# Query-key products of a chunked RWKV-7 block on Trainium2: two column tiles of 64 keys, or four of up to 32

## What is computed

```python
xn = layernorm(x)
# r, w, k, v, kk, a from xn by mixing with the row before, projections and low-rank terms
def step(S, inp):                       # S: 64 x 64 state
    rt, dt, kt, vt, at, bt = inp        # at = -kk, bt = kk * a, dt = exp(w)
    sa = einsum('bhij,bhj->bhi', S, at)
    S = S * dt[:, :, None, :] + sa[..., None] * bt[:, :, None, :] + vt[..., None] * kt[:, :, None, :]
    y = einsum('bhij,bhj->bhi', S, rt)
    return (S, y)
y = groupnorm(scan(step)) * ln_w + ln_b + bonus(r, k, v)
s = (y * g) @ w_output.T
out = x + s * silu(ffn(xn))
```

## Time and profile before

| | us |
|---|---|
| median of 3 runs | 1610.01 |
| lowest, highest | 1604.13, 1610.34 |
| span of the profiled execution | 1603.4 |
| TensorE matmuls busy in it | 1520.5 |
| TensorE weight loads busy | 1064.9 |
| VectorE busy | 1243.6 |
| ScalarE busy | 1069.5 |
| GpSimd busy | 354.6 |

### The profile page before, as it was taken

One profiled execution on the slowest core, in us unless ns is written; L12 is line 12 of the kernel. 1 busy time (PEld: TensorE's weight loads), 2 busy tenths in 40 slices (PEclk: granted clock), 3 DMA queues, 4 the chain that ended last, 5 costly groups with the idle time before them and its releaser, 6 DMA issues.

```text
span 1603.4 us, 48245 instructions
## 1 busy us (share of the span) xinstructions
PE 1520.5 (95%) x20288; PEld 1064.9 (66%) x20288; DVE 1243.6 (78%) x2661; ACT 1069.5 (67%) x1889; POOL 354.6 (22%) x362
## 2 busy tenths in 40 slices
PE   3699999999999999999999999999999999999887
PEld 1366767576676757667676676757667675766765
DVE  2968787787878878887887878778787887888643
ACT  3758586685857758685775858668585775768512
POOL 3121402313040131302213140231304013130201
PEclk9799999999999999999999999999999999999999
DMA  4011110301212021111202111030121202111020
GB/s 149 14 25 29 33 34 16 62 18 32 43 25 47 16 55 25 33 34 24 56 16 39 42 34 34 16 62 19 33 42 25 48 16 55 25 33 34 12 56 28
DMA packets 251430, 57.85 MB, mean 36 GB/s; under 512 B 223696, under 2 KB 250704, under 8 KB 251088
## 3 DMA queue, kind: packets, MB, share of 16 engines
q1 hardware_dynamic: 241936, 41.95, 13.9%
q10 hardware_dynamic: 9280, 12.81, 2.2%
HBM read 36.38 MB, written 18.35 MB: 34 GB/s over the span
## 4 chain that ended last, share of the span: by engine, by line
PE 92%; DVE 3%; ACT 2%; issue 1%; POOL 0%; DMA 0%; SPq 0%; ACTq 0%; DVEq 0%; POOLq 0%
PE bank L534 23%; PE chunk L380 15%; PE bank L544 11%; PE bank L509 8%; PE bank L664 4%; PE chunk L642 3%; PE chunk L614 3%; PE chunk L589 3%; PE chunk L598 2%; PE bank L485 2%; PE bank L380 2%; PE bank L517 2%; PE bank L479 2%; PE chunk L628 2%; DVE VU L981 1%
## 5 line engine op out<-in xcount | busy, mean ns | idle before, releaser
L1325 POOL TENSOR_TENSOR SF<-ST,CT 128x256 f32<-128x256 f32 x128 | 99.7, 779 | 728.8 <-DVE ST L1211 728.8
L534 PE MATMUL bank<-xT,wg 128*128 128x256 f32 x768 | 197.2, 391 | 14.2 <-DVE VU L981 13.5
L534 PE MATMUL bank<-xT,wu 128*128 128x256 f32 x768 | 207.3, 395 | 0.0
L544 PE MATMUL bank<-wd,hT 128*128 128x256 f32 x768 | 176.8, 383 | 1.9 <-DVE hT L1171 1.9
L534 PEld LDWEIGHTS bank<-xT,wg 128*128 128x128 f32 x768 | 136.3, 189 | 57.6 <-DVE VU L981 24.1
L544 PEld LDWEIGHTS bank<-wd,hT 128*128 128x128 f32 x768 | 143.3, 190 | 29.3 <-issue 7.2
L534 PEld LDWEIGHTS bank<-xT,wu 128*128 128x128 f32 x768 | 135.1, 188 | 34.8 <-issue 14.5
L380 PE MATMUL chunk<-KS,W 128*128 128x512 f32 x320 | 149.6, 598 | 0.3 <-ACT gT L719 0.3
L509 PE MATMUL bank<-qpad,KS 128*64 128x32 f32 x4096 | 141.2, 226 | 4.0 <-DVE KE L1143 4.0
L887 ACT ACTIVATE Y<-chunk 32x256 f32<-32x256 f32 x256 | 96.3, 376 | 70.9 <-PE chunk L598 67.0
L509 PEld LDWEIGHTS bank<-qpad,KS 128*64 128x64 f32 x4096 | 130.7, 141 | 14.1 <-issue 9.0
(11 more groups left out here) (156 smaller groups left out, 3231.3 us busy)
## 6 DMA issues: line engine op xcount, KB each, us to landing
smalls<-in_x SPq DMA_DIRECT2D x32, 256.0 KB, 3.1
Y<-in_x SPq DMA_DIRECT2D x32, 256.0 KB, 3.0
out<-fsil ACTq DMA_DIRECT2D x32, 256.0 KB, 2.6
scrA<-AM SPq DMA_DIRECT2D x64, 64.0 KB, 1.9
hat<-scrB SPq DMA_DIRECT2D x32, 128.0 KB, 3.1
hat<-scrF SPq DMA_DIRECT2D x32, 128.0 KB, 3.1
KE<-scrA SPq DMA_DIRECT2D x64, 32.0 KB, 2.2
scrT<-KE SPq DMA_DIRECT2D x16, 128.0 KB, 1.7
```

The source lines that it names most:

```text
L534: q = pe.matmul(o[:, TT_ * n2:TT_ * n2 + TT_], w[:, h, 128 * (n + n2):128 * (n + n2) + 128], x_now[:, h], start=(h == 0), stop=(h == NH - 1))
L544: q = pe.matmul(o[:, 256 * m:256 * m + 256], hT[:, n, 128 * m:128 * m + 128], wd[:, n, :], start=(n == 0), stop=(n == NF - 1))
L1325: pool.tensor_tensor(SF[:, :, :, :], ST[:, :, :, :], fade[:, c].unsqueeze(3).to_broadcast([128, B, NH, N]), ALU.mult).then_inc(*faded.up)
```

## The change

Each product is split by kind of key. Instead of one with 64 weight columns there are two, x = 0 and x = 1, whose results start at partitions 64b and 64b + 32: four column tiles of the array instead of two. Each loads only the keys up to the end of its query group, 8, 16, 24 or 32 columns, where 64 were loaded before. Streamed columns, the result's place in PSUM for every entry that the mask lets through, the mask and the order strings are as before. Result rows beyond the loaded keys are no longer written and keep what the bank held; the mask drops them.

```diff
-                                oc = o[64 * b:64 * b + 64, 128 * n:128 * n + 128].rearrange("p (x e) -> p x e", e=L)
-                                q = pe.matmul(oc[:, :, BL * j:BL * j + BL], K[:, 2 * n + b, 64 * j:64 * j + 64],
-                                              Q[:, 2 * n + b, j, :, :, :].rearrange("p a b e -> p (a b) e"), start=True, stop=True)
+                                for x in range(2):
+                                    p0, keys = 64 * b + L * x, BL * j + BL
+                                    oc = o[p0:p0 + keys, 128 * n:128 * n + 128].rearrange("p (x e) -> p x e", e=L)
+                                    q = pe.matmul(oc[:, :, BL * j:BL * j + BL], K[:, 2 * n + b, 64 * j + L * x:64 * j + L * x + keys],
+                                                  Q[:, 2 * n + b, j, :, :, :].rearrange("p a b e -> p (a b) e"), start=True, stop=True)
```

## The result

The changed kernel takes 1629.4 us (median of 4 runs, 1626.8 to 1646.8) where the kernel before takes 1610.2 beside it: ratio 1.0155, 95% interval 1.0123 to 1.0186. It is 1.5% slower (the ratios here compare the means of the runs, so they can differ by a few tenths of a per cent from the ratio of the medians, 1.012 in this case). The forecast was 1581, 1.8% faster, with a range of 1561 to 1602. The profiled execution took 1631.2 us, 1629.7 of it span, 26.3 more than the profiled one of before.

What follows compares the result with a forecast made beforehand. TensorE, 92% of the chain, was taken as the bound, its waves set by 64-column loads. Fourteen middle sections gave 26.6 us, the last 1.6, the first 1: 29 off 1610.0 gives 1581 us, range 1561 to 1602.

Steps and rivals of the forecast that it cites:

- the 58 ns: Products before the change: each wave of two starts takes 58 ns, set by loading 64 weight columns, 0.83 ns each.
- The wave after: Changed products: four tiles run together, 32 ns a wave; a half takes 0.64 us, a turn 1.15.
- the one for all tiles together: Matmul starts: 25 ns minimum taken across all tiles, 1.6 us per half, a kernel some 85 us slower.
- Rival D: Changed products: four column tiles over one row group don't run at once; 1622 or 1638 us, chance 0.12.
- Rival A: Short loads and streams: a fixed time per tile keeps waves between 32 and 58 ns; 1590 to 1604 us, chance 0.16.
- The walk: One middle section, followed through PE's waits for ACT and DVE: 1.9 us of 3.4 saved comes through.
- I take 0 in the sum: Fetching and issuing 8192 more instructions: priced at 0, with bounds of 0 and 0.9 us per half.
- C: Rival, changed products: nothing gained, wave near 58 ns by issue or half-overlapping tiles; 1604 to 1616 us, chance 0.07.
- The row of 32 starts: Two interleaved groups at 634.94 to 635.39: 32 starts in 0.45 us, taken to prove 64 instructions in that time.
- The trace shows no bound on that: Instruction fetch and issue: no limit seen against a half needing 128 instructions in 0.64 us instead of 64 in 1.06.
- the raw gain: Shorter halves and turns before waits: 3.4 us per tile of rows, 54 us over 16.
- The signs that were to show it: 8192 starts on L511, shorter halves, PE idle before L630, L591, L519 (0.1 to 0.5 us), sections 1.9 us shorter.

Runs made afterwards that it cites:

- v_trim64: Kernel before, still two column tiles, loading only key columns up to the mask's edge of kind 1 (40, 48, 56 or 64 instead of 64): 1592.1 us, ratio 0.9883.
- e_kind0: Changed kernel with only kind 0's products, kind 1's left out and its mask rows cleared, so the result is not the reference's: 1582.0 us, ratio 0.9831.
- a_after: The changed kernel, unaltered, measured a second time on another chip: 1641.3 us, ratio 1.0203 of the kernel before.

## Why the prediction was wrong, point by point

**What bounds the kernel, and the 58 ns: right.** A load's columns set the wave above 32 columns (v_trim64: 0.89 us a half, as computed from 0.83 ns a column).

**The wave after: right.** Waves of four start 29 to 32 ns apart in the first half shown above (their first starts at 640.127, .159, .188, .217), where 32 was forecast; a half takes 0.67 us at the median of the undisturbed ones (forecast 0.64), a turn 1.35 (forecast 1.15, partly by waits: the shortest is 1.21). Four column tiles over the same rows do run side by side, with starts 7 to 8 ns apart. Of the two readings of the Trainium skill's 25 ns between starts (TensorE: Matmul & The Clock Gate, section "Wait — 56ns, not 53.3ns?"), the one for all tiles together is refuted here. Rival D, that the tiles do not overlap, is refuted too, though the time fell into its range: its place was the array, and the array was fast. Rival A, a floor per tile between 32 and 58 ns, is also out.

**The walk and its sum of 29 us: right where the instructions allow it.** e_kind0, with about the array time of the forecast and the old number of instructions, takes 1582.0 us against the 1581 forecast, is 25 us (by the ratio 27) faster than its kernel before against 29 forecast, gains 1.9 us a section, and has its leads within 0.07 us of the walk's at each of the six places. Its halves were 0.05 us shorter than forecast and it uses two tiles, so it tests the walk and the waits, not the overlap of four tiles, which the halves of the changed kernel show.

**"I take 0 in the sum": the step that failed.** It stands under "What else is edited", as the price of 8192 more instructions, with bounds of 0 and 0.9 us per half, from 64 instructions seen in 0.45 us. What it cost was 38.3 us of standstills, and by the balance below some 10 us more at half clock behind them, against a gain of 27; the upper bound, "near no saving", was too low as well, and among the rivals only C named issue, with nothing gained at most (1604 to 1616). The row of 32 starts proves how fast instructions that are already there can be issued. It says nothing of how fast new ones arrive: 64 instructions are a quarter of a piece, and the limit is one piece in 2.7 to 3.7 us, some 11 to 14 ns an instruction, over a stretch of several us. "The trace shows no bound on that" was wrong as well. The q8 row was there (162 packets of 16.4 KB), and so were two idle times of 0.35 us ended by "issue" in the middle of groups, each after a piece that had been used up in 3.3 to 3.4 us. The kernel before ran just at the edge: four of its pieces pass in under 3.4 us; of after's, 52 do.

**The balance.** Against the profiled execution of before, in us of span: the array's gain as e_kind0 shows it, 1.9 a section, -27; 32 standstills, +38.3; half clock, 34.4 us instead of 14.0 after the first 95, at most half of the difference, +10 (an estimate); and the start, which was 4.3 us later in this execution before the first product of the change had run (L494, the last TensorE group ahead of them, stands at 72.01 instead of 67.72):

```profile
72.01 1.98 PE L494 MATMUL bank<-KS,con 64*64 64x512 f32 x8 [7.77 <-DVE KS L1062]
```

Together +26, measured 26.3 (L494 stands at 67.7 to 74.6 us in the twelve profiled executions, and before's is the earliest). This adds terms as if they did not touch one another, which is rough: while TensorE stands, the other engines get ahead, and a part of the waits that ate the raw gain in e_kind0 falls away. Behind the third half TensorE is idle before L591 for 0.14 us in after, 15 times, and for 0.25 us in e_kind0; before L519 it is 0.32 at most against 0.45.

The medians differ by only 19 us and the means by 25. Before's profiled execution, the early starter, was 6.6 us under its median, and after's was 1.8 us over.

**The signs that were to show it.** 8192 starts on L511, DVE and ACT unchanged: seen. New idle times before L591 and L519: seen, but smaller than forecast (0.14 us and up to 0.32), and none before L630 that before did not have. Each section 1.9 us shorter: not seen, the median is 96.2 us against 95.1.

## What to carry to other kernels

Where a change splits tensor instructions into more and shorter ones, count the instructions that pass in any 3.5 us, not only those of a group: here TensorE got 256 in 2.7 to 3.7 us, and what the array saved beyond that came back, and more, as standstills in the middle of groups, put down to "issue". First take the saving that adds no instruction (here the shorter load, which kept 1.2%), and split only where long instructions stand around. Tiles of one width belonged together here.

## What the runs showed of the hardware that I had not expected

- TensorE's instructions arrive in pieces of 256, each by one packet of 16.4 KB (0.9 to 1.9 us, 1.05 at the median in after), and a piece used up in 1.2 us is followed by a standstill of 1.8 us, one used up in 3.3 us by 0.3 us.
- Several of these standstills are followed by 3.4 or 6.8 us at a granted clock of 0.50, 1.2 GHz: six of after's, from 1.0 to 1.5 us after TensorE had started again, all behind standstills of 1.3 us or more, but not behind each of these (13 others of 1.28 us or more had none). In a_after it also fell in the middle of two, of 2.37 and 1.96 us. The two profiled executions of this one kernel had 34 and 61 us at 0.50, and spans of 1629.7 and 1641.3.
- A change of the column tiles' width, from four of up to 16 to two of 56 or back, takes 123 to 152 ns from the last start of the one to the first of the other, and avoiding two of them saved 0.24 us. I measured these two directions only, and don't know which part of it is waiting for the tiles before to drain.
- Four column tiles over all 128 rows take float32 products at one wave of four per 29 to 32 ns.
